# A fused cross-attention and feed-forward kernel: in each group of two units TensorE issues the jobs before the probability products

## What is computed

```python
def xattn(q, k, v):
    qh = split_heads(q @ Wq.T + bq) / sqrt(16)
    kh, vh = split_heads(k @ Wk.T + bk), split_heads(v @ Wv.T + bv)
    attn = softmax(einsum('bhqd,bhkd->bhqk', qh, kh), axis=-1)
    return merge_heads(einsum('bhqk,bhkd->bhqd', attn, vh)) @ Wo.T + bo

x = x + xattn(layernorm(x), ctx, ctx)            # x, ctx: (8, 512, 256) fp32
h1 = einsum('gmh,goh->gmo', layernorm(x), W1) + b1   # W1: (8, 1024, 256)
x = x + einsum('gmo,gho->gmh', h1, W2) + b2          # W2: (8, 256, 1024)
```

## Time and profile before

| | |
|---|---|
| time, median of 3 runs | 616.38 us (615.13 to 617.40) |
| span of the profiled execution | 613.0 us |
| its own time | the span and 3.4 us around it, if it was as long as the median run |
| TensorE matmuls busy | 584.0 us, 95% of the span |
| TensorE weight loads busy | 296.0 us, 48% |
| DVE busy | 458.9 us, 75% |
| ACT busy | 397.0 us, 65% |
| POOL busy | 221.2 us, 36% |
| share of the chain that ended last | PE 83%, ACT 7%, issue 3%, others 7% |

### The profile page before, as it was taken

One profiled execution on the slowest core, in us unless ns is written; L12 is line 12 of the kernel. 1 busy time (PEld: TensorE's weight loads), 2 busy tenths in 40 slices (PEclk: granted clock), 3 DMA queues, 4 the chain that ended last, 5 costly groups with the idle time before them and its releaser, 6 DMA issues.

```text
span 613.0 us, 11485 instructions
## 1 busy us (share of the span) xinstructions
PE 584.0 (95%) x3380; PEld 296.0 (48%) x3380; DVE 458.9 (75%) x854; ACT 397.0 (65%) x746; POOL 221.2 (36%) x298
## 2 busy tenths in 40 slices
PE   7899989999999999999999999999999999889997
PEld 7545323545454544545444544445445454335457
DVE  5698787878888778787888777878788788786124
ACT  4217776776767586776667776676767766776741
POOL 5011028213660148212570138411481146313721
PEclk9969999999999999999999999999999999999999
DMA  8730333263224614254132823256042622260100
GB/s 291 186 93 2 86 90 105 54 215 115 81 62 131 213 40 140 54 194 133 45 95 55 264 61 117 47 161 189 8 137 53 208 54 76 66 208 2 69 21 34
DMA packets 34076, 65.23 MB, mean 106 GB/s; under 512 B 9778, under 2 KB 11642, under 8 KB 31994
## 3 DMA queue, kind: packets, MB, share of 16 engines
q1 hardware_dynamic: 34042, 64.81, 35.6%
HBM read 34.65 MB, written 4.44 MB: 64 GB/s over the span
## 4 chain that ended last, share of the span: by engine, by line
PE 83%; ACT 7%; issue 3%; POOL 2%; DVE 2%; DMA 1%; SPq 1%; ACTq 0%; DVEq 0%; POOLq 0%
PE st L449 20%; PE misc L471 20%; PE pv L463 18%; PE misc L549 11%; PE nat L439 8%; ACT probs L728 4%; PE misc L481 2%; ACT hi L748 1%; PE nat L430 1%; DMA bq_in<-bq 1%; PE misc L530 1%; ACT normedT_hi L741 1%; PE nat L471 1%; ACT normedT_hi L734 0%; POOL b_part L1185 0%
## 5 line engine op out<-in xcount | busy, mean ns | idle before, releaser
L896 DVE TENSOR_REDUCE neg_max<-nat 128x1 f32<-128x512 f32 x512 | 330.5, 679 | 78.9 <-PE nat L439 77.9
L728 ACT ACTIVATE probs<-st 128x512 f32<-128x512 f32 x505 | 283.3, 597 | 161.8 <-PE st L449 156.9
L449 PE MATMUL st<-qs,ks 64*128 64x512 f32 x505 | 200.9, 461 | 18.7 <-ACT probs L728 18.6
L439 PE MATMUL nat<-ks,qs 63*128 63x512 f32 x512 | 208.1, 471 | 1.9 <-DMA qs<-hi 1.1
L463 PE MATMUL pv<-probs,vs 128*32 128x512 f32 x1024 | 136.4, 605 | 0.0
L449 PEld LDWEIGHTS st<-qs,ks 64*128 64x128 f32 x505 | 80.5, 185 | 112.0 <-ACT probs L728 73.6
L439 PEld LDWEIGHTS nat<-ks,qs 63*128 63x128 f32 x512 | 83.4, 187 | 11.8 <-DVE neg_max L896 7.0
L549 PE MATMUL misc<-w_in 128*128 128x256 f32 x256 | 80.7, 411 | 0.0
L1147 POOL TENSOR_TENSOR pair_ctx<-pair_ctx,inv_sum 128x512 f32<-128x512 f32 x15 | 19.1, 1276 | 118.7 <-DMA inv_sum<-inv_dram 118.7
L549 PEld LDWEIGHTS misc<-w_in 128*128 128x128 f32 x256 | 40.6, 189 | 42.9 <-issue 35.5
L463 PEld LDWEIGHTS pv<-probs,vs 128*32 128x32 f32 x1024 | 20.1, 108 | 38.7 <-issue 35.8
(11 more groups left out here) (168 smaller groups left out, 803.5 us busy)
## 6 DMA issues: line engine op xcount, KB each, us to landing
w_in<-w SPq DMA_DIRECT2D x8, 1024.0 KB
w_in<-w2T SPq DMA_DIRECT2D x8, 1024.0 KB
ks<-hi SPq DMA_DIRECT2D x64, 128.0 KB, 2.4
qs<-hi SPq DMA_DIRECT2D x64, 128.0 KB, 2.5
x_in<-x SPq DMA_DIRECT2D x8, 512.0 KB, 3.4
ctx_in<-ctxT SPq DMA_DIRECT2D x8, 512.0 KB, 4.3
ks<-lo SPq DMA_DIRECT2D x32, 128.0 KB, 2.4
qs<-lo SPq DMA_DIRECT2D x32, 128.0 KB, 2.6
```

The lines of the kernel that those rows point to most:

```text
L439: mm(nat_of(n)[:, :], qs[rows, 2 * g + jj, c * P:(c + 1) * P], ks[rows, 2 * g + jj, :], start=True, stop=True).then_inc(nat_done, 1)
L449: mm(st_of(u, prep)[:, :], ks[rows, 2 * g + jj, kc * P:(kc + 1) * P], qs[rows, 2 * g + jj, :], start=True, stop=True).then_inc(st_done, 1)
L728: act.activation(probs[kc % 2][:, j, :], st_of(u, prep)[:, :], ACT.Exp).then_inc(exp_done, 1)
L896: dve.tensor_reduce(neg_max[:, g % 2, at:at + 1], nat_of(n)[:, :], AX.X, ALU.max, negate=True).then_inc(max_done, 1)
```

## The change

In TensorE's `turn`, the loop that issues the jobs of both units of a group moves from behind the `pv` block to in front of it. The conditions, the waits inside each piece and all other engines stay as they are.

```diff
--- before.py
+++ after.py
@@ -638,13 +638,13 @@
                         st(b, u, prep)
                         for row, n in nats_of(b, u, post, prep):
                             nat(row, n)
+                    for u in (u0, u0 + 1):
+                        jobs(b, u, post, prep)
                     if u0 % 4 == 2:
                         if u0 > 4:
                             pv(b, u0 // 4 - 1)
                         elif post:
                             pv(b - 1, 15)
-                    for u in (u0, u0 + 1):
-                        jobs(b, u, post, prep)
 
             pe.wait_ge(pool_set, 3)
             pe.wait_ge(dve_set, 1)
```

## The result

The changed kernel takes 627.34 us (median of 4 executions, 625.93 to 634.34), the kernel before on the same chip 616.89 us. The ratio is 1.017, with a 95% interval of 1.010 to 1.025: slower, as forecast. The forecast was 627.5 us.

A forecast was written before the change was run, and what follows sets the result against it. TensorE's own queue was taken to set the time. Uncovered waits of 5.8 + 3.1 + 1.0 + 1.2 = 11.1 us, added to 616.4, gave 627.5 us, with a range of 621.5 to 631.5.

The forecast's parts named there:

- The work itself: TensorE's instructions in every group with jobs: only their order changes, passage from job to pv free, so 0 us.
- Place C: Unit 39: job yT waits for ACT's copy w_half, 0.79 us late in turns 1 to 6, 1.03 in turn 7; 5.8.
- Place A: Units 3 to 9: late pv delays odd_sum, pair_ctx, row maximum, nat by 0.89, 0.37 given back; 3.1 us.
- Place B: Unit 15: the key job waits for DVE's first normedT_lo copy, 0.15 us in turns 0 to 6; 1.0 us.
- Place D: Units 51 to 55: w21 job delays pv, even_sum and exps, st of unit 55 0.17 us later; 1.2 us.
- The waits of units 3 and 31: w21_ready and y_ready, met shortly before TensorE arrives: costed at nothing, with 0.3 us a turn left for slips.
- ACT's even_sum at unit 19 finds ACT idle until exp 20: Unit 19: a later pv was to hold up nothing on ACT; costed at nothing.
- The other jobs' waits, all of which end before `pv` starts in this trace: Jobs elsewhere in the turn: their inputs were to be ready in the new position too; costed at nothing.
- The rival that the delays are taken back: Later TensorE finds exps done; three quarters or more of 11.1 us come back, 616.4 to 619.2 us; chance 0.09.

The follow-up runs named there:

- second profile: The changed kernel run once more, unaltered: ratio 1.016 (1.006 to 1.025) to the kernel before, span 627.0 us.
- place C alone: The kernel before with jobs first only in the group of units 38 and 39: ratio 1.007 (1.002 to 1.012).
- early copy: The changed kernel with ACT's copy w_half behind exp 37 instead of exp 38: 622.75 us, ratio 1.013 to the kernel before.
- the cut at DVE: The changed kernel with DVE making pair_ctx behind the row maximum of unit 4 instead of unit 3: ratio 1.020 to the kernel before.
- the late mask: The kernel before (pv first) with ACT making even_ctx behind exp 26 instead of exp 22: ratio 0.992 (0.987 to 0.996).
- two fillers: The late mask kernel plus two unused 128-column matmuls behind each of 18 start-up score products: ratio 0.999 to the kernel before.

## Why the prediction was right

The forecast, 627.5 us, and the measured 627.34 agree more closely than the runs could separate: the interval of the ratio spans 6 to 15 us of loss. The last 0.2 us are luck. The sharper test is the second profile: less the 2.4 us of its start-up its span is 624.6, and the forecast for it was 613.0 + 11.1 = 624.1. What carried it, by its own steps:

- **The work itself at nothing**: shown. The passage from job to `pv` takes 0.21, and eleven groups swapped alone cost 0.10 a turn, most of it a wait at unit 23. Out of a job it takes 0.20 to an `st` and 0.21 to `pv`, against 0.11 inside the job: about 0.1 for the change of shape, whichever comes next. And `pv`'s weight load isn't pulled under the job (262.42, with its matmul). Of the two rules of the Trainium skill that the prediction set against each other, that of "TensorEngine Tiling (Array Packing)", Key Properties, says that a change of the tiling mode drains the engine. The runs agree with it.
- **Place C, 0.79**: measured 0.79 to 0.80, and 0.98 in turn 7 where 1.03 were forecast; shown by swapping that group alone and by removing the wait alone.
- **Place A, 0.89 and 0.37 given back**: measured 0.89 and 0.35 in turns 2 to 5. The chain through odd_sum, pair_ctx and the row maximum is shown by cutting it at DVE, which left 0.07 of the 0.89.
- **Place B, 0.15**: measured 0.14 in turns 2 to 5 and 0.27 to 0.29 in turns 1 and 6, which the prediction took to be like turn 3. They aren't: there `pv` stood 0.24 ahead of the end of the copy, and 0.09 in turn 3. Turn 0 had 0.09. It is a term mis-sized by 0.2 us in all.
- **Place D, 0.17**: measured 0.18 in turns 2 to 5, and 0.10 in the others. For B and D the mechanism rests on the rows and on their showing wherever their groups are swapped; neither was swapped alone or cured.
- **The waits of units 3 and 31, at nothing with 0.3 a turn for slips**: nothing came out there in turns 1 to 6.
- **"ACT's even_sum at unit 19 finds ACT idle until exp 20", costed at nothing**: wrong by a little. The projection job of unit 19 takes 0.9 us, and even_sum came so late that exp 20 had to wait for it. ACT's `hi` and DVE's `lo` follow that exp, and 0.08 to 0.09 a turn came out at unit 23, where `maxT` had lost its cover. "The other jobs' waits, all of which end before `pv` starts in this trace" was true of the trace, but this one ends later after the change.
- **The time behind it**: the terms gave 9.8 us for turns 1 to 6, measured were 10.1; turn 7 was given 1.0, its part at unit 38 was 0.98, and 0.9 more came at units 22 to 25 in this execution (0.6 in the second profile), behind a transfer that took longer; why it did is open.

The rival that the delays are taken back held only where the prediction itself had put it, at unit 9. Elsewhere in turns 1 to 6 no group became shorter by 0.05 us; the kernel with place C alone shows it cleanly.

## What to carry to other kernels

In this kernel, where TensorE's queue hardly ever runs dry, the order of two pieces of work was free only as long as the inputs of the first were there and nobody waited for the second. Work whose inputs are always ready is worth most directly behind a point at which other engines have just been given something to do, as cover for what waits on them; so put it ahead of the jobs that need a fresh result. To price a reordering, compare for each moved wait the end of its releaser with the start of what stands there now, one row each, and then follow what the displaced piece releases: here 0.9 us came out on an engine (DVE) that the diff doesn't touch.

## What the runs showed of the hardware that I had not expected

Executions of one and the same kernel differ by up to 11 us (spans of 612.7 to 623.8 in 29 of the kernel before), and the mean granted clock goes with it, from 0.989 down to 0.969. In the profiles the difference lies before turn 0, which began between 42.2 and 49.5 us where the start-up code was the same, with the clock at its lower level, 1.2 GHz, for 7 to 27 us of the start-up. In the kernel before it fell at 34 us: from 30 to 42.45 us TensorE is "busy" for 11.66 of 12.45 by the trace, yet each `nat` comes only when DVE's row maximum releases it, every 0.60 us; with two filler matmuls in the same place the mean clock was 0.994 or more in all ten executions. In the three profiles whose turn 0 began latest (48.0 to 49.5) it fell earlier, at 26 us, where no filler stands: TensorE had waited 1.2 to 1.4 us for a transfer shortly before (`nat` for `qs`), but it did so in the kernel before as well, for 1.1. The clock fell again in turn 7, for 3.4 us between units 42 and 46, in five of the kernels: place C alone, the early copy, the cut at DVE, the late mask and two fillers. In the kernel with the early copy:

```profile
572.00:577.00 5.00, 3.94 (x23) 1.46 (x27) 1.83 (x4) 3.81 (x9) 4.69 (x6) 1.00 0.02 5
577.00:578.50 1.50, 1.50 (x10) 0.29 (x2) 0.00 (x0) 0.37 (x1) 1.34 (x3) 0.65 0.02 6
578.50:580.00 1.50, 1.50 (x9) 1.47 (x8) 0.00 (x0) 1.09 (x2) 1.34 (x3) 0.50 0.07 11
```

Behind a stretch in which the engine was busy for 3.94 of 5.00 us the clock fell to its lower level, job matmuls followed each other at 0.21 instead of 0.12, and the turn grew by 1.3 us at unit 44. The five microseconds before the same point of the kernel before (566.33 to 571.33) have 4.04 busy, and those of the changed kernel's second profile (580.4 to 585.4) 3.52, and there the clock stayed up. The 1.3 us are more than place C costs in a turn, and whoever compares two kernels by a few executions should look at the clock of the profile first.
